# Joining the state-space and the feed-forward stage of a two-layer sequence model into one block of engine programs

## What is computed

```python
# layer 0
mod = t @ Wm + bm                         # six vectors: shift_a, scale_a, gate_a, shift_ff, scale_ff, gate_ff
y_mod = ln(y) * (1 + scale_a) + shift_a
y = y + gate_a * s5(y_mod)                # state-space: project in (B_bar), scan over tokens, project out (C), + D*u
scale_c, shift_c = split(t @ Wc + bc)
y_mod = (ln(y) * (1 + scale_c) + shift_c) * (1 + scale_ff) + shift_ff
y = y + gate_ff * (gelu(y_mod @ W1 + b1) @ W2 + b2)     # W1 512 x 2048, W2 2048 x 512
# layer 1
h = sln(y); q, k, v = h @ Wqkv.T + bqkv   # 16 heads of 32
out = (softmax(q @ k.T) / sqrt(512) @ v) @ Wp.T + bp
h1 = out + y; result = sln(h1) + h1
```

## Time and profile before

| | us |
|---|---|
| median of 3 runs (lowest, highest) | 3131.61 (3124.97, 3133.08) |
| the profiled execution, its own time | 3128.11 |
| its span, first to last instruction | 3126.0 |
| PE busy, share of the span | 2981.7 (95%) |
| DVE busy | 2031.5 (65%) |
| POOL busy | 1715.1 (55%) |
| ACT busy | 1510.5 (48%) |

### The profile page before, as it was taken

How to read it: one execution, slowest core, us unless ns; L and a number is a source line. 1 busy time by engine, 2 the same in 40 slices (tenths; PEclk the granted TensorE clock), 3 DMA queues, 4 the chain that set the end, 5 groups by cost and what they waited for, 6 DMA issues and landing times. The chain is left out here.

```text
span 3126.0 us, 41762 instructions
## 1 busy us (share of the span) xinstructions
PE 2981.7 (95%) x15298; PEld 1946.8 (62%) x15298; DVE 2031.5 (65%) x3598; ACT 1510.5 (48%) x2743; POOL 1715.1 (55%) x711
## 2 busy tenths in 40 slices
PE   4897999999998899999999999999999999999987
PEld 2785888878887687755555555555555555555456
DVE  7864322232221656678888888888888888888438
ACT  3532232232332222156666666666666666666634
POOL 2764210111110111148888888888888888888834
PEclk8898999999999899999999999999999999999989
DMA  6433100000000446374557754576554767454457
GB/s 230 141 137 120 41 28 1 27 28 27 27 14 15 175 179 206 135 177 102 106 119 157 156 117 103 118 153 141 126 115 99 157 131 154 100 120 99 97 191 279
DMA packets 143661, 363.24 MB, mean 116 GB/s; under 512 B 10934, under 2 KB 28858, under 8 KB 126952
## 3 DMA queue, kind: packets, MB, share of 16 engines
q1 hardware_dynamic: 125322, 228.50, 23.9%
q0 software_dynamic: 18144, 132.13, 20.9%
HBM read 144.25 MB, written 83.92 MB: 73 GB/s over the span
## 5 line engine op out<-in xcount | busy, mean ns | idle before, releaser
L1672 ACT ACTIVATE probs<-psum 128x512 f32<-128x512 f32 x2048 | 1053.2, 610 | 576.7 <-PE psum L1591 574.0
L1788 POOL TENSOR_TENSOR pair<-probs 128x2048 f32<-128x2048 f32 x255 | 1179.9, 4627 | 261.0 <-ACT probs L1672 250.0
L1698 DVE TENSOR_REDUCE part_max<-psum 128x1 f32<-128x512 f32 x1984 | 1218.5, 680 | 104.9 <-PE psum L1576 102.7
L1591 PE MATMUL psum<-queries,keys 97*128 97x512 f32 x2048 | 848.5, 416 | 5.3 <-ACT probs L1672 2.8
L1576 PE MATMUL psum<-keys,queries 96*128 96x512 f32 x1984 | 801.9, 405 | 3.0
L1591 PEld LDWEIGHTS psum<-queries,keys 97*128 97x128 f32 x2048 | 386.0, 189 | 341.2 <-issue 213.3
L1603 PE MATMUL psum<-probs,values 128*32 128x512 f32 x4096 | 494.2, 600 | 0.0
L1576 PEld LDWEIGHTS psum<-keys,queries 96*128 96x128 f32 x1984 | 376.2, 190 | 126.6 <-DVE part_max L1698 49.7
L983 DVE TENSOR_TENSOR h_lo<-w_stage,h_hi 128x512 fp32r<-128x512 f32 x128 | 99.7, 779 | 516.8 <-ACT h_hi L918 516.8
L911 ACT ACTIVATE w_stage<-psum,b_col 128x512 f32<-128x512 f32 x128 | 88.4, 690 | 499.1 <-PE psum L38 497.7
L1603 PEld LDWEIGHTS psum<-probs,values 128*32 128x32 f32 x4096 | 107.0, 109 | 234.2 <-ACT probs L1672 135.9
(11 more groups left out here) (312 smaller groups left out, 3758.7 us busy)
## 6 DMA issues: line engine op xcount, KB each, us to landing
pair<-pair POOLq DMA_DIRECT2D x126, 1024.0 KB, 7.3
queries<-q_parts SPq DMA_DIRECT2D x96, 256.0 KB, 4.8
keys<-k_parts SPq DMA_DIRECT2D x42, 512.0 KB, 7.4
x<-in_x_dram SPq DMA_DIRECT2D x8, 1024.0 KB, 7.6
y<-in_x_dram SPq DMA_DIRECT2D x8, 1024.0 KB, 6.0
y_rows<-y SPq DMA_DIRECT2D x8, 1024.0 KB, 4.4
qkv_z<-z_rows SPq DMA_DIRECT2D x8, 1024.0 KB, 5.7
q_parts<-qk_hi SPq DMA_DIRECT2D x32, 256.0 KB, 2.0
```

Of the source, the lines that this page charges most:

```text
L1591: nc.tensor.matmul(psum[:, SC + unit % 3, :], keys[place(count)[0]][0:R + 1, h, kt * P:(kt + 1) * P], queries[count % NQ][0:R + 1, h, :], ...
L1672: act.activation(probs[tile % NPROB][:, h, :], psum[:, SC + unit % 3, :], ACT.Exp).then_inc(exp_ready, 1)
L1698: dve.tensor_reduce(part_max[:, h * TT + qt, kc:kc + 1], max_slot(), AX.X, ALU.max).then_inc(max_read, 1)
L1788: pool.tensor_tensor(pair[number % NPAIR][:, :, :], probs[2 * number % NPROB][:, :, :], probs[(2 * number + 1) % NPROB][:, :, :], ALU.add) ...
```

## The change

The two stages return one function for each engine instead of opening a block, and the caller runs both in one block, one after the other on each engine. In detail:

- **The ninth chunk.** The state-space loops treat `y_first` as chunk 8: DVE's moments and inversion stand in step 6, ACT's normalisation in step 6 and its modulation (with the feed-forward gain and shift) in step 7, PE's transposes in step 7, POOL's four low parts in step 7. The same tiles `norm`, `u_hi[2]`, `u_lo[2]` then serve the feed-forward loop. `y_first` is loaded at step 3 instead of step 7.
- **Weights ahead.** ACT writes the high part of (1,0) at the end of step 6, DVE its low part at the start of step 7; SP then loads (2,0) into the freed tile. Only two pieces of W1 are loaded ahead, not three.
- **Behind the hand-over.** ACT still splits the high part of (2,0), DVE its low part. All six other pieces go to POOL, both parts each, in the order (1,1), (1,2), (2,1), (2,2), (1,3), (2,3).
- **Hand-over.** ACT, DVE, POOL and SP wait for the last `cy_ready`, `y_ready`, `shi_ready` and `slo_ready` before their feed-forward part; PE waits for the ninth chunk's u_lo only, and then for `g_ready` and `ulo_ready`, which ACT and DVE raise behind that wait. Nobody waits for the last stores of y any more, except before their tiles are written again.
- **Memory.** `wm` is six tiles of 512 columns instead of one, five of them lent by later stages, loaded by six DMAs whose rows are 2 KB instead of three with rows of 4 KB. W1 and W2 parts are one tile for each piece.

```diff
-def prep_stage(nc, sb, sem, psum, a, ident, columns, s5, x, wgb, vec_dram):
+def prep_stage(nc, sb, sem, psum, a, ident, columns, s5, x, wgb, lent, vec_dram):
-    wm = sb("wm", [P, KT, 6 * D])
+    wm = lent + [sb("wm_last", [P, KT, D])]
...
-            for n in range(3):
-                cols = slice(2 * n * D, 2 * (n + 1) * D)
-                sp.dma_start(wm[:, :, cols], a["L0_cond_Wm"].rearrange("(k p) n -> p k n", p=P)[:, :, cols]).then_inc(ld_wm[n], 16)
+            for n in range(6):
+                sp.dma_start(wm[n][:, :, :], a["L0_cond_Wm"].rearrange("(k p) n -> p k n", p=P)[:, :, n * D:(n + 1) * D]).then_inc(ld_wm[n // 2], 16)
...
-                    pe.wait_ge(ld_wm[0], 16)
-                    pe.wait_ge(ld_wm[1], 16)
+                    pe.wait_ge(ld_wm[0], 32)
+                    pe.wait_ge(ld_wm[1], 32)
...
+    def sync(sp):
...
+        for piece, tile in enumerate(w1_stage[:2]):
+            sp.dma_start(tile[:, :, :], a["L0_cond_W1"].rearrange("(k p) f -> p k f", p=P)[:, :, piece * D:(piece + 1) * D]).then_inc(w1_ld, 16)
+        for c in range(STEPS):
...
+            if c == B + 1:
+                sp.dma_start(y_first[:, :, :], rows(y_dram, 0)).then_inc(y_first_ld, 16)
+            if c == STEPS - 1:
+                sp.wait_ge(wlo_dve, 1)
+                sp.dma_start(w1_stage[0][:, :, :], a["L0_cond_W2"].rearrange("(f p) d -> p f d", p=P)[:, 0:KT, :]).then_inc(w_ld[0], 16)
...
+        turn(0, range(KT))
+        for c in range(STEPS):
+            project_in(c)
+            turn(c + 1, (0, 1))
+            if c > 0:
+                project_out(c - 1, (0,))
+            turn(c + 1, (2, 3))
+            if c > 0:
+                project_out(c - 1, range(1, TT))
+        project_out(STEPS - 1, range(TT))
...
+            if c + 2 <= STEPS:
+                take_root(c + 2)
+            modulate(c + 1)
+            if c + 2 <= STEPS:
+                normalise(c + 2)
+            split_state(c)
+            if c == STEPS - 2:
+                act.wait_ge(norm_ready, TT * STEPS)
+                act.wait_ge(w1_ld, 32)
+                act.activation(ahead["w1_hi"][:, :, :], w1_stage[0][:, :, :], ACT.Copy).then_inc(whi_ready, 1)
...
+            if c + 2 <= STEPS:
+                moments(c + 2)
+                invert(c + 2)
+            else:
+                dve.wait_ge(whi_ready, 1)
+                dve.tensor_tensor(ahead["w1_lo"][:, :, :], w1_stage[0][:, :, :], ahead["w1_hi"][:, :, :].bitcast(F32), ALU.subtract).then_inc(wlo_dve, 1)
...
+        for c in range(STEPS):
+            turn(c)
+            split(c + 1, (0, 1))
+            turn_back(c)
+            split(c + 1, (2, 3))
+            split_state(c)
+
+    def finished(engine):
+
+        engine.wait_ge(cy_ready, TT * STEPS)
+        engine.wait_ge(y_ready, TT * STEPS)
+        engine.wait_ge(shi_ready, 2 * STEPS)
+        engine.wait_ge(slo_ready, 2 * STEPS)
...
-    HI_ACT = [(1, 0), (1, 1), (1, 3), (2, 0)]
-    LO_DVE = [(1, 0), (1, 1), (2, 0)]
-    POOL = [(1, 3), (2, 1), (1, 2), (2, 2), (2, 3)]
-
-    HELD = [[(1, 0), (2, 0), (1, 2), (2, 2), (2, 3)], [(1, 1), (2, 1)], [(1, 3)]]
-    LOADS = [(2, 0), (2, 1), (1, 2), (2, 2), (2, 3)]
+    HI_ACT = [(1, 0), (2, 0)]
+    LO_DVE = [(1, 0), (2, 0)]
+    POOL = [(1, 1), (1, 2), (2, 1), (2, 2), (1, 3), (2, 3)]
+
+    HELD = [[(1, 0), (2, 0), (1, 2), (2, 2), (1, 3), (2, 3)], [(1, 1), (2, 1)]]
+    LOADS = [(1, 2), (2, 1), (2, 2), (1, 3), (2, 3)]
...
+    def scalar(act):
+        state_space["finished"](act)
+        act.sem_inc(u_ready, KT + 2)
+        act.sem_inc(root_ready, 1)
+        act.sem_inc(g_ready, 2)
...
+        split_high(*HI_ACT[1])
+        act.wait_ge(consts, 1)
...
+        dve.wait_ge(b1_tp, 1)
+        dve.tensor_copy(b1_col[:, :], psum[:, ACC, 0:FT]).then_inc(consts, 1)
+
+        for w, p in LO_DVE[1:]:
+            split_weight(w, p)
+        dve.wait_ge(gate_ld, 32 * B)
+        for b in range(B):
+            dve.tensor_tensor(lift[b][:, :], lift[b][:, :], gate[b][:, :], ALU.mult).then_inc(lift_ready, 1)
...
+        state_space["finished"](pool)
+        for n, (w, p) in enumerate(POOL):
+            wait_loaded(pool, w, p)
+            if w == 2 and p >= NP - B:
+                state_space["stored"](pool, p - (NP - B))
+            pool.tensor_copy(part(w1_hi, w2_hi, w, p), raw(w, p)).then_inc(whi_pool, 1)
+            pool.wait_ge(whi_pool, n + 1)
+            split_low(pool, w, p, wlo_pool)
```

More of the change, by code:

```diff
@@ L402, in s5_stage @@
     u = [sb(f"u{n}", [P, CH]) for n in range(2)]
-    u_hi, u_lo = ([sb(f"u_{part}{n}", [P, KT, CH], F32R) for n in range(NU)] for part in ("hi", "lo"))
+    u_hi, u_lo = ([sb(f"u_{part}{n}", [P, KT, CH], F32R) for n in range(NU - 1)] + [ahead[f"u_{part}"]] for part in ("hi", "lo"))
     prod = sb("prod", [P, 4, CH])
@@ L419, in s5_stage, with chunk_in @@
     TR, BU, CY = 0, 2, 6
+    def chunk_in(c):
+        return x[c % B] if c < STEPS else y_first
     def rows(dram, c):
@@ L701, in ffn_stage @@
+def ffn_stage(nc, sb, sem, psum, a, ident, columns, state_space, ahead, stage, y_first, vec_dram, y_dram, z_dram):
+    NP = 4
+    FP = FT // NP
+    w1_hi, w1_lo = ([ahead[f"w1_{n}"]] + [sb(f"w1_{n}{p}", [P, KT, FP * P], F32R) for p in range(1, NP)] for n in ("hi", "lo"))
+    w2_hi = [sb(f"w2_hi{p}", [P, FP, D], F32R) for p in range(NP - B)] + ahead["w2_hi"]
+    w2_lo = [sb(f"w2_lo{p}", [P, FP, D], F32R) for p in range(NP)]
     y = [y_first, stage[1]]
-    norm = sb("ffn_norm", [P, TT, D])
+    norm = ahead["norm"]
@@ new lines, in sync, with store @@
+    def sync(sp):
+        state_space["finished"](sp)
+        sp.sem_inc(y_ld[0], 16)
+        for b in range(B):
+            sp.dma_start(gate[b][:, :], vec_dram[V_GATE_F, b:b + 1, :].broadcast_to((P, D))).then_inc(gate_ld, 16)
+            sp.dma_start(lift[b][:, :], a["L0_cond_b2"].rearrange("(o d) -> o d", o=1).broadcast_to((P, D))).then_inc(gate_ld, 16)
+        for w, p in LOADS:
+            tile, before = held(w, p)
+            wait_split(sp, *HELD[tile][before - 1])
+            sp.dma_start(raw(w, p), source(w, p)).then_inc(w_ld[tile], 16)
+            if (w, p) == (2, 2):
+                wait_split(sp, *HELD[1][-1])
+                sp.dma_start(y[1][:, :, :], chunk(y_dram, 0, 1)).then_inc(y_ld[1], 16)
+        wait_split(sp, *HELD[0][-1])
+        for b in range(B):
+            state_space["stored"](sp, b)
+        sp.dma_start(stage[0][:, :, :], wqkv_rows(a)[0]).then_inc(wq_ld, 16)
+        def store(i, b):
+            sp.wait_ge(z_ready, TT * (2 * i + b + 1) + Z_FREE)
+            sp.dma_start(chunk(z_dram, i, b), y[b][:, :, :]).then_inc(z_st[b], 16)
+        with sp.Fori(0, NCH - 1) as i:
+            for b in range(B):
+                store(i, b)
+                sp.wait_ge(z_st[b], 16 * (i + 1))
+                sp.dma_start(y[b][:, :, :], chunk(y_dram, i + 1, b)).then_inc(y_ld[b], 16)
+        for b in range(B):
+            store(NCH - 1, b)
+        for b in range(B):
+            sp.wait_ge(z_st[b], 16 * NCH)
+        sp.wait_ge(wq_ld, 16)
```

892 lines of the change are left out of this document (413 added, 479 removed).

## The result

Over seven executions the changed kernel takes 3111.26 us (median; 3101.19 to 3116.11), the kernel before, beside it on the same chip, 3129.03. The ratio is 0.9943, with a 95% interval from 0.9931 to 0.9954: 17.8 us less, where 3116 was forecast (range 3104 to 3126). The profiled execution took 3114.0 us with a span of 3112.2 (before: 3128.1 and 3126.0). In a later set of runs the same kernel gave 0.9942.

What follows compares the result with a forecast made beforehand. PE, busy for 95% of the span, was taken as the bound, so only its idle or slow time could be gained. +0.6 - 17.5 + 2.6 = -14.3 us gave 3113.8 or 3117.3, taken as 3116, range 3104 to 3126.

Steps and rivals of the forecast that it cites:

- Hand-over: Between state-space stage and feed-forward: DVE held by POOL, first `down` at F+11.3 = 258.1 against 275.57, -17.5 us.
- F: End of the state-space stage, DVE's last add: forecast to move from 244.09 to 246.8 (245.1 to 248.4).
- Rival 1: Behind the state-space end, DVE runs between POOL's instructions, first `down` at F+6.7 or F+5.8: 3107; chance 0.15.
- Step 7: Last state-space step: POOL's s_lo ends later, +1.0 us; half-speed clock behind PE's idle time, +1.7 (0 to +3.3).
- Preparation: Start of the kernel: Wm's 2 KB rows load more slowly, all passed to the end, +0.6 us (0 to +1).
- Rival 3: At the start, a 2 KB row of Wm costs as much as 4 KB, 14 to 21 us later: 3137; chance 0.05.
- Slow clock behind the first `down`: After PE's idle time there, matmuls start at the 1.2 GHz level: +2.6 us (+1.7 to +3.3).
- late h_lo: Feed-forward loop: POOL's five low parts can each delay an h_lo by up to 4.9 us; net 0 (-0.9 to +2).
- the rest of the loop is PE's own: Feed-forward loop from the first `down`: PE in steady order, one DVE delay there having cost it 0.85 us.
- No wait for a weight piece: Feed-forward loop: POOL's pieces are ready before PE needs them, the tightest with 7.6 us to spare.
- Rival 2: Most is given back: PE waits again, likely for h_lo behind POOL's low parts or for gate loads: 3124; chance 0.17.

Runs made afterwards that it cites:

- pool_waits: Changed kernel, with POOL's first low part, of (1,1), waiting for DVE's first h_lo: 3109.11 us, ratio 0.9938.
- before_u_first: Kernel before, with the feed-forward's u_hi and u_lo laid at the start of its memory instead of near its end: 3122.34 us, ratio 0.9982.
- lifts_and_order: Changed kernel, POOL's first low part waiting for the first h_lo and the lifts moved from DVE to POOL behind its last piece: 3108.25 us, ratio 0.9937.
- lifts_early: Changed kernel, POOL's first low part waiting for the first h_lo and the lifts on POOL right behind that part: 3109.28 us, ratio 0.9930.
- lifts_on_pool: Changed kernel, with the two multiplications of lift by gate moved from DVE to POOL, behind POOL's last weight piece: 3108.63 us, ratio 0.9938.

## Why the prediction was right

The sign, the size (3111 against 3116) and the main term were right; one term was missing, and the loss by the slow clock was forecast too large twice. One by one:

- **Hand-over**, first `down` at F+11.3: it came at F+11.1, in two executions. The mechanism was the one named, POOL's low part first, then DVE's, the lifts, h_lo. DVE's low part took 6.46 us with POOL beside it and 2.29 without. The Trainium skill, page "SBUF — State Buffer", section "SBUF: two separate sides", has the rule that VectorE and GpSimd share a port pair as an exclusive lock; these two times agree with it. Some luck is in the last tenths: the last load of b2, which the forecast had landing by F+8.4 (its issue until F+2.4, then at most 6.0), let the lifts begin only at F+9.1, 0.21 us behind the end of the hold. Rival 1 (DVE not held, 3107) fell by the 6.46. It would most likely not have brought its 7 us either: with the hold gone in pool_waits the lifts waited for that load until F+11.3, and the first `down` came at F+13.4.
- **Step 7** (s_lo +1.0, slow clock +1.7): s_lo ended 16.0 us behind DVE's first product, where 16.1 was forecast, and without a slow stretch F came 1.1 us later behind that product than in the one profile of the kernel before (27.3, 26.2). The slow stretch was mis-sized: it came in four of eight profiles, 1.2 us each, 0.6 on the mean. The forecast also took the step of the one profile before for the rule: its five forms take 24.6 to 27.8, by how long the clock is low in them. From mean to mean step 7 grew from 26.5 to 27.9, +1.4 in place of +2.7, from few executions.
- **Preparation** (+0.6): not seen for certain. PE's first group of projections starts at 19.7 on the mean in the four forms of the kernel before that load Wm as ever and at 20.1 in the nine of the changed one, with 1.6 to 2.0 us between executions. DVE's first product of step 7 starts at 216.8 in the same four and at 216.4 in the nine, and executions differ by 3.6. Rival 3 (slower, by Wm's rows) fell by the same numbers.
- **Slow clock behind the first `down`** (+2.6) **and late h_lo** (0, -0.9 to +2): the chunk from the first `down` to its last gated product takes 92.0 us where it took 89.5 (349.02 - 257.07, 365.03 - 275.57): +2.5. The clock is less than forecast, 5 us at 0.66 lose 1.7. The h_lo are more: 2.2 us of waits in this chunk against 0.8, so +1.4. That makes +3.1; if this chunk too runs 0.9 us faster by the rate of the loop (next point), which no experiment shows by itself, +2.2 are left, near the 2.5. No wait for a weight piece, as forecast.
- **What the forecast lacked is the loop.** It held that "the rest of the loop is PE's own" and took its length as given. But PE's matmuls read tiles, the change moved u from one end of the memory to the other, and seven chunks became 6.0 us shorter. That is a third of the whole gain and stood in no term and no rival. before_u_first shows it in the kernel before; u was not moved back in the changed one, but the chunk lengths are the same, 90.81 and 90.80. Without it the change is worth 12 us (17.8 - 5.9), where the sum had 14.3.

In the pair of profiled executions the sum looks better than it was: -13.8 against -14.3, the 6.0 of the loop and 8.2 of chance behind it having taken each other away.

Rival 2 (given back by an h_lo held behind POOL's pieces) did not come in the changed kernel, but it is real: lifts_and_order and lifts_early lose 3.5 and 4.8 us by it, where POOL's last piece and DVE's chain for the next chunk meet.

## What to carry to other kernels

When work comes earlier on one engine, ask what else it now runs beside: here the earlier start that two edits gave together was lost 60 us later, where the last piece that POOL splits met DVE's chain of short operations, and it counted only with one more wait that kept the two apart. A change that moves tiles in SBUF changes the rate of the matmuls that read them, so compare the length of a steady stretch first, and test placement by itself. Read terms of a microsecond from several executions; one profile has them by chance.

## What the hardware did that was not expected

- **A matmul's rate depends on where its operands lie in a partition.** With u_hi and u_lo at 197,760 and 205,952 bytes, a group of 16 `up` and 16 `down` tiles takes 91.73 us; with them at 50,016 and 58,208, or at 66,400 and 74,592, 90.81; with h and W2 below 140,128 as well, 89.35. W1's row length (8 KB or 2 KB) makes no difference (91.74). Whether it is the low address, or the distance from what ACT and DVE write at the same time (h from 218,816, ffn_u from 193,664 in the kernel before), is open.
- **DVE's short operations are held too**, also those with one tensor operand: the TENSOR_SCALAR of line 77, four elements per partition, took 1.22 us beside POOL's additions (lifts_early), where it takes 0.17. In lifts_early four of the six links of that chain took about 1.2 us, the time of one of POOL's additions, one took 4.37, and one was not held.
- **The clock behind a short idle time is not certain.** The same wait of 1.65 us was followed by a stretch at 0.66 in four executions and by full clock in four; in two of these last four the stretch came 12 us later, behind a wait of 1.02, in the other two not at all. In the kernel before, the wait of 1.35 us in step 7 was followed by a low clock in four of five forms and by full clock in one.
- **Small loads landed later beside a large one**: the two of b2, 256 KB each, took 5.7 us from issue to landing in the changed kernel and 6.0 in lifts_on_pool, but 6.9 in pool_waits and 6.3 in lifts_and_order, where SP issued a load of 1 MB sooner, right behind them. No experiment changed that load alone, so the cause is not shown.
